# Two attention stages of a twelve-stage decoder: where TensorE sends the turned results and the turned maxima

## The chip, the cores and the metric

The program runs on one core of a Trainium2 chip. Five engines of the core are used: TensorE (matrix products, into PSUM), VectorE, ScalarE, GpSimd, and SyncE, which issues most of the DMAs. Each works through its own list of instructions in order and waits at semaphores. PSUM has eight banks of 128 x 512 words. The metric is the device time of one execution, in microseconds (us); 4994.01 is the median of three runs, from 4988.22 to 5001.19.

## The reference, cut to what matters

Twelve sub-layers follow one another, each added to x and normalized. The change touches the eighth (cross-attention to a memory, with a key mask) and the eleventh (attention over the context and x's own tokens). Both take queries from x (8 batches of 256 tokens, 128 features):

```python
def _L2_xattn_ref(memory, query, seq_mask, b):      # 8 heads of 16
    ...
    logits = jnp.einsum('bhqd,bhkd->bhqk', Q, K) + b[0]
    logits = logits + -1e+30 * (1.0 - mask)
    weights = jax.nn.softmax(logits, axis=-1)
    out = jnp.einsum('bhqk,bhkd->bhqd', weights, V)

def _L3_xattn_ref(x, context, w_qkv, w_proj, b_proj):  # 16 heads of 8
    ...
    k = jnp.concatenate([extra_k, k], axis=2)
    v = jnp.concatenate([extra_v, v], axis=2)
    attn = jnp.einsum('bhnd,bhmd->bhnm', q * scale, k).astype(jnp.float32)
    attn = jax.nn.softmax(attn, axis=-1).astype(dtype)
    out = jnp.einsum('bhnm,bhmd->bhnd', attn, v)
    return out.transpose(0, 2, 1, 3).reshape(B, N, C) @ w_proj.T + b_proj
```

The memory and the context are the same array of 1601 rows per batch. So there are 1601 keys in the first of the two and 1601 + 256 = 1857 in the second.

## The kernel before, in words

Every stage of the program ends before the next begins. Both attention stages are run by one class, `KeyMajorAttention`; below they are called memory (stage 7) and crossself (stage 10). Heads are taken in groups of four: 16 groups in memory, 32 in crossself.

A group has two parts. The first finds the largest score of each query, so that the softmax can subtract it. TensorE computes the scores with the queries on the partitions, and VectorE reduces them along the keys. That is cut into 24 *looks* per group (`pe_look`, L2315, and `dve_look`, L2462, L2465, L2469). An even look takes a slice of keys of two heads into PSUM banks 4 and 5; an odd look takes what is left of one head or of both into bank 7. After a group's 24th look VectorE splits the maxima into three parts of lower precision (`dve_split`, L2476 to L2485); TensorE *turns* them, so that they lie in rows (`pe_turn_max`, L2343, into bank 7); ScalarE copies the rows out (`act_rows`, L2425); and SyncE sends them by DMA into the stack of queries (`sp_rows`, L2289).

The second part goes over the keys in *steps* of 128: 13 steps in memory, 15 in crossself. In a step TensorE computes the scores of four heads with the keys on the partitions, the negated maxima included (`pe_scores`, L2369); ScalarE takes the exponential (L2444); TensorE multiplies with V and a column of ones (`pe_values`, L2388), summing over the steps in bank 6. After the last step ScalarE copies the sums (`act_take`, L2432), TensorE turns them back (`pe_back`, L2353, two products into bank 7), and VectorE divides and writes the result (`dve_out`, L2494 and L2495).

The looks of one group run among the steps of the group before. `looks_by(half)` says how many looks have been sent by a half step, 36 at the start, then 24 per group. In a step TensorE sends the scores of step u, some looks, the product with V of step u - 1, and some looks. In crossself a step has one or two looks (24 in 15 steps), in memory two in most.

Three things share bank 7: the odd looks, the turned maxima and the turned results. `wait_misc` (L2331) makes TensorE wait, before it writes there, until ScalarE has copied the last turned maxima and VectorE has taken the last turned result. `pe_turn_max` and `pe_back` also wait until VectorE has reduced the last odd look (`alone_done`). A look waits until VectorE has reduced the one two before it.

TensorE turns the maxima of group g at the end of the step `turn_step(g)`, and the result of group g at the end of step (g + 1) x steps + 2, each behind that step's looks. VectorE takes the turned result at the end of the same step, and ScalarE copies the turned maxima behind the exponential of step `turn_step(g)`.

Of the kernel before, what the change touches and what calls it, by code (L numbers as in the profile page):

```python
# [36 lines left out]
class Chain:  # L37


    def __init__(self, eng, sem):  # L40
        self.eng, self.sem, self.n = eng, sem, 0
# [157 lines left out]
class GroupNorm:  # L199
# [22 lines left out]
    def run_dve(self, dve, link, take):  # L222
        for g in range(4):
            if take:
                link(take(g))
            for t in range(4 * g, 4 * g + 4):
                ins = dve.bn_stats(self.stats[:, t, :], self.x[:, t, :])  # L227
            link(ins)
            for t in range(4 * g, 4 * g + 4):
                ins = dve.bn_aggr(self.moments[:, t, :], self.stats[:, t, :])  # L230
            link(ins)
            c = slice(4 * g, 4 * g + 4)
            dve.tensor_scalar(self.var[:, c], self.moments[:, c, 1], self.eps, None, ALU.add).then_inc(self.var_ready, 1)
            if g:
                self.dve_scale(dve, link, g - 1)
        self.dve_scale(dve, link, 3)
        for t in range(self.by_act, NT):
            dve.tensor_scalar(self.x[:, t, :], self.x[:, t, :], self.moments[:, t, 0:1], self.rstd[:, t:t + 1],
                              ALU.subtract, ALU.mult).then_inc(self.normed_dve, 1)
# [42 lines left out]
    def run_pe(self, pe, banks):  # L282
        if self.last:
            return
        for g in range(4):
            self.wait_normed(pe, g)
            for t in range(4 * g, 4 * g + 4):
                ins = pe.transpose(self.env.ps[:, banks[g], (t % 4) * P:(t % 4 + 1) * P], self.x[:, t, :],
                                   self.env.ident[:, :])
            ins.then_inc(self.turned, 1)  # L290
# [1891 lines left out]
class KeyMajorAttention:  # L2182


    def __init__(self, st, heads, hd, rows, lanes, tiles, nk, out_of):


        self.env, self.nc, self.ps = st.env, st.nc, st.env.ps
        self.heads, self.hd, self.rows, self.lanes, self.tiles, self.nk, self.out_of = (heads, hd, rows, lanes, tiles,
                                                                                       nk, out_of)  # L2190
        self.steps = len(tiles)
        self.per_batch = heads // 4
        self.groups = B * self.per_batch
        self.looks = 24
        self.lead = 12
        self.moves = lanes
        self.units = self.groups // lanes
        c = -(-2 * nk // 9)
        self.both = [(i * c, (i + 1) * c) for i in range(3)]
        self.alone, self.left_over = (3 * c, 4 * c), (4 * c, nk)  # L2200
        self.kst = st.sb("kst", [P, 4, 4, nk], BF16)
        self.qst = st.sb("qst", [P, 4, 4, S], BF16)
        self.v = st.sb("v", [P, 2, self.steps, D])
        self.vh = st.sb("vh", [P, 2, self.steps, heads, hd + 1])
        self.prob = st.sb("prob", [P, 3, 4 * S])
        self.oT = st.sb("oT", [P, S])
        self.part_max = st.sb("part_max", [P, 2, 8, 5])
        self.nmax = st.sb("nmax", [P, 8])
        self.left = st.sb("left", [P, 8])
        self.parts = st.sb("parts", [P, 24], BF16)  # L2210
        self.max_rows = st.sb("max_rows", [32, P], BF16)
        self.rsum = st.sb("rsum", [P, 2, 4])
        self.ones = st.sb("ones", [32, nk], BF16)
        names = ("ones_ready", "ones_loaded", "v_loaded", "v_ready", "stacks_loaded", "s_ready", "s_free", "split_ready", "turned_max",
                 "rows_ready", "max_loaded", "st_ready", "exp_done", "pv_done", "o_copied", "back_turned", "out_done",
                 "bank_clear", "dve_own")
        self.sem = {n: st.sem(n) for n in names}
        self.ident_h = st.sb("ident_h", [P, P], BF16)

    def base(self, h):  # L2220
        return 64 * (h % 2) if self.lanes == 2 else 0
# [16 lines left out]
    def turn_step(self, g):  # L2238

        return g * self.steps - self.lead * self.steps // self.looks + 2  # L2240


    def run_pool(self, pool, spans):
# [148 lines left out]

    def run_pe(self, pe):
        total = self.groups * self.steps
        turns = {self.turn_step(g): g for g in range(1, self.groups)}
        backs = {(g + 1) * self.steps + 2: g for g in range(self.groups - 1)}
        self.turned = self.backed = 0
        pe.wait_ge(self.sem["ones_loaded"], 4 * 2 * 16)
        for n in range(self.looks):
            self.pe_look(pe, n)  # L2400
        self.pe_turn_max(pe, 0)
        for n in range(self.looks, self.looks_by(0)):
            self.pe_look(pe, n)
        for u in range(total):
            self.pe_scores(pe, u)
            for n in range(self.looks_by(2 * u), self.looks_by(2 * u + 1)):
                self.pe_look(pe, n)
            if u:
                self.pe_values(pe, u - 1)
            for n in range(self.looks_by(2 * u + 1), self.looks_by(2 * u + 2)):  # L2410
                self.pe_look(pe, n)
            if u in turns:
                self.pe_turn_max(pe, turns[u])
            if u in backs:
                self.pe_back(pe, backs[u])
        self.pe_values(pe, total - 1)
        self.pe_back(pe, self.groups - 1)

# [80 lines left out]
    def run_dve(self, dve):  # L2499
        s = self.sem  # L2500
        link = Chain(dve, s["dve_own"])
        dve.tensor_copy(self.ident_h[:, :], self.env.ident[:, :])
        dve.memset(self.ps[:, 6, :], 0.0).then_inc(s["bank_clear"], 1)
        dve.wait_ge(s["bank_clear"], 1)
        total = self.groups * self.steps
        backs = {(g + 1) * self.steps + 2: g for g in range(self.groups - 1)}

        def look(n):
            self.dve_look(dve, n)
            if n % self.looks == self.looks - 1:  # L2510
                self.dve_split(dve, link, n // self.looks)
        for n in range(self.looks_by(0)):
            look(n)
        for u in range(total):
            for n in range(self.looks_by(2 * u), self.looks_by(2 * u + 2)):
                look(n)
            if u in backs:
                self.dve_out(dve, link, backs[u])
        self.dve_out(dve, link, self.groups - 1)


# [1949 lines left out]
```

## Time and profile before

| | |
|---|---|
| median of three runs | 4994.01 us |
| profiled execution | 4985.95 us |
| its span, from first to last instruction | 4984.1 us |
| mean granted clock of TensorE | 0.890 of full speed |
| TensorE busy | 4023.9 us (81%), 29194 products |
| VectorE busy | 3487.3 us (70%) |
| ScalarE busy | 2467.5 us (50%) |
| GpSimd busy | 1335.3 us (27%) |
| L2315 on TensorE, the looks | 431.3 us, 1920 products |
| L2388 on TensorE, products with V | 430.7 us, 5504 records |
| L2369 on TensorE, scores | 345.9 us, 2752 products |
| L2462 on VectorE, even looks | 564.7 us, 576 instructions |
| L2444 on ScalarE, exponentials | 703.9 us, 688 instructions |

The shares are over all twelve stages. The rows further down are cut to the two stages: memory runs from about 3380 to 3760 us after the start, crossself's attention from about 4180 to 4830. A line's time is busy time, whether it lies on the path that sets the end or not; what an engine stands for is shown in brackets behind its next instruction.

### The profile page before, as it was taken

How to read it: one execution, taken by the hardware profiler on the slowest of the kernel's cores; microseconds unless marked ns; L12 is line 12 of the kernel's file. 1: busy time of each engine (PE TensorE's matmuls, PEld its weight loads, DVE VectorE, ACT ScalarE, POOL GpSimd, SP SyncE). 2: the span in 40 equal slices, each digit the busy share in tenths (PEclk: the TensorE clock that was granted, in tenths of full speed). 3: DMA queues.
4: the chain of work that ended last, by engine and by line, in shares of the span. 5: the costliest groups of instructions: out<-in, count | busy, mean ns of one | idle time of the engine just before them, and what ended most of it. 6: DMA issues, size and time to landing. Idle time of an engine off the chain costs nothing. (4 is left out here: it accounts for less than half of the span.)

```text
span 4984.1 us, 77257 instructions
## 1 busy us (share of the span) xinstructions
PE 4023.9 (81%) x29194; PEld 2215.1 (44%) x29259; DVE 3487.3 (70%) x5453; ACT 2467.5 (50%) x3477; POOL 1335.3 (27%) x984
## 2 busy tenths in 40 slices
PE   5640787999999999999986995866996677888883
PEld 3630345666666666666653332432443342222231
DVE  6569554777777777777774445766774558888868
ACT  2120224666666666666652223543664354777772
POOL 0000001656666665666675203000000100000000
PEclk5565898999999999999997996987997688999996
DMA  0010510000000000000004106315650333323200
GB/s 19 1 53 0 105 60 27 1 14 14 1 14 1 14 1 14 1 14 1 1 1 154 37 0 152 54 15 102 86 80 4 91 59 64 56 49 56 49 2 9
DMA packets 145927, 184.01 MB, mean 37 GB/s; under 512 B 21562, under 2 KB 110156, under 8 KB 144932
## 3 DMA queue, kind: packets, MB, share of 16 engines
q1 hardware_dynamic: 137860, 162.65, 15.8%
q0 software_dynamic: 6528, 16.42, 1.4%
q8 instruction: 233, 3.82, 0.3%
q14 instruction: 122, 1.00, 0.1%
q10 hardware_dynamic: 1184, 0.12, 0.0%
HBM read 141.04 MB, written 35.08 MB: 35 GB/s over the span
## 5 line engine op out<-in xcount | busy, mean ns | idle before, releaser
L2993 POOL TENSOR_TENSOR arena<-arena 128x512 f32<-128x512 f32 (+1 forms) x768 | 1132.7, 1477 | 692.0 <-ACT arena L2949 638.7
L2444 ACT ACTIVATE arena<-ps 128x1024 f32<-128x1024 f32 (+1 forms) x688 | 703.9, 1024 | 313.1 <-PE ps L2369 302.6
L2462 DVE TENSOR_REDUCE arena<-ps 128x2 f32<-128x826 f32 (+1 forms) x576 | 564.7, 980 | 165.9 <-PE ps L2315 157.5
L3009 DVE TENSOR_TENSOR arena<-arena 128x1024 f32<-128x1024 f32 (+1 forms) x448 | 646.6, 1482 | 13.9 <-ACT arena L2976 13.9
L3031 DVE TENSOR_TENSOR arena<-ps,arena 128x512 f32<-128x512 f32 (+1 forms) x768 | 530.1, 690 | 177.3 <-ACT arena L2943 144.3
L2315 PE MATMUL ps<-arena 48*128 48x413 bf16 (+3 forms) x1920 | 431.3, 330 | 130.2 <-DVE arena L2462 65.7
L2943 ACT ACTIVATE arena<-ps 128x1024 f32<-128x1024 f32 (+1 forms) x448 | 410.5, 960 | 205.2 <-PE ps L2871 193.5
L2855 PE MATMUL ps<-arena 128*128 128x256 f32 (+1 forms) x1664 | 444.0, 392 | 20.6 <-DVE arena L3017 19.3
L2949 ACT ACTIVATE arena<-arena 128x1024 f32<-128x1024 f32 (+1 forms) x448 | 424.9, 992 | 50.8 <-DVE arena L3009 48.3
L2388 PE MATMUL ps<-arena 128*9 128x256 f32 (+2 forms) x5504 | 430.7, 384 | 11.4 <-ACT arena L2432 8.5
L2871 PE MATMUL ps<-arena 64*128 64x256 f32 (+1 forms) x3328 | 427.6, 391 | 5.6 <-ACT arena L2965 1.3
L2885 PE MATMUL ps<-arena 128*64 128x256 f32 (+1 forms) x3328 | 411.6, 388 | 7.1 <-ACT arena L2949 7.1
L2847 PE MATMUL ps<-arena 128*128 128x400 f32 (+1 forms) x1024 | 400.6, 514 | 2.9 <-ACT arena L2971 2.8
L2871 PEld LDWEIGHTS ps<-arena 64*128 64x128 f32 (+1 forms) x3328 | 301.4, 182 | 149.7 <-issue 94.8
L2855 PEld LDWEIGHTS ps<-arena 128*128 128x128 f32 (+1 forms) x1664 | 282.4, 185 | 154.5 <-issue 61.4
L2369 PE MATMUL ps<-arena 51*128 51x256 bf16 (+3 forms) x2752 | 345.9, 274 | 1.8 <-DMA arena<-arena 1.7
L2315 PEld LDWEIGHTS ps<-arena 48*128 48x128 bf16 (+1 forms) x1920 | 126.4, 95 | 453.0 <-DVE arena L2462 231.4
L2885 PEld LDWEIGHTS ps<-arena 128*64 128x64 f32 (+1 forms) x3328 | 220.4, 137 | 172.2 <-issue 85.3
L2263 POOL COPY arena<-arena 128x1536 f32<-128x1536 f32 (+2 forms) x40 | 30.1, 786 | 909.7 <-DMA arena<-arena 502.3
L2965 ACT ACTIVATE arena<-ps 128x400 f32<-128x400 f32 (+1 forms) x256 | 129.4, 506 | 257.0 <-PE ps L2847 257.0
L2847 PEld LDWEIGHTS ps<-arena 128*128 128x128 f32 x1024 | 182.6, 190 | 127.3 <-ACT arena L2971 14.2
L3041 DVE RECIPROCAL arena<-ps 128x256 f32<-128x256 f32 x64 | 112.5, 1757 | 151.8 <-PE ps L2926 151.8
(637 smaller groups left out, 5710.1 us busy)
## 6 DMA issues: line engine op xcount, KB each, us to landing
arena<-ctx_parts SPq DMA_DIRECT2D x96, 200.1 KB
arena<-ctx_parts SPq DMA_DIRECT2D x192, 100.1 KB
arena<-fs_rows SPq DMA_DIRECT2D x128, 128.0 KB, 4.1
arena<-in_ctx_feat SPq DMA_DIRECT2D x8, 1601.0 KB, 6.4
arena<-in_ctx SPq DMA_DIRECT2D x16, 768.0 KB
arena<-diff_att_stack SPq DMA_DIRECT2D x60, 192.0 KB
ctx_parts<-arena SPq DMA_DIRECT2D x24, 400.2 KB, 3.5
arena<-in_w SPq DMA_DIRECT2D x1, 6416.0 KB, 18.4
```

Of the source, the lines that this page charges most:

```text
L2315: return pe.matmul(self.ps[:, bank, c0:c0 + hi - lo], self.qst[r0:r1, ring, self.slot(g, h), q * P:(q + 1) * P], self.kst[r0:r1, ring, sel ...
L2388: ins = pe.matmul(self.ps[32 * k:32 * k + self.hd + 1, 6, 0:S], self.vh[0:rows, b % 2, t, h0 + k, :], self.prob[0:rows, u % 3, k % 2 * 2 * ...
L2444: act.activation(self.prob[0:rows, u % 3, :], self.ps[0:rows, 2 * (u % 2):2 * (u % 2) + 2, :].rearrange("p n c -> p (n c)"), ACT.Exp).then ...
L2462: ins = dve.tensor_reduce(dst[:, :, j // 2], self.ps[:, 4:6, 0:hi - lo], AX.X, ALU.max)
L2847: ins = pe.matmul(ps[:, bank, 0:hi - lo], W("wk")[:, half * INNER + u % HP * P:half * INNER + u % HP * P + P], ctxT[:, u // HP % 2, half, ...
L2855: ins = pe.matmul(ps[0:rows, bank, 0:2 * P], ctxT[:, g // 4 % 2, half, c0:c0 + rows], W("wv")[:, half * INNER + g % 4 * 2 * P:half * INNER ...
L2871: ins = pe.matmul(ps[0:rows, 2 + 2 * (s % 2) + e, t % 2 * S:(t % 2 + 1) * S], kT[e * HW:(e + 1) * HW, u % 2, c0:c0 + rows], q[e * HW:(e + ...
L2885: ins = pe.matmul(ps[e * HW:(e + 1) * HW, 6 + u % 2, 0:S], v[0:rows, u // 2 % 2, t, c0:c0 + HW], sc[0:rows, u % 2, t, e * S:(e + 1) * S], ...
L2949: act.activation(e, e, ACT.Exp).then_inc(exp_done, 1)
L2993: pool.tensor_tensor(acc[0:rows, u % 2, :], before, sc[0:rows, u % 2, t, :], ALU.add).then_inc(added, 1)
L3009: dve.tensor_tensor(e, e, mb[0:rows, u % 2, None, :].to_broadcast([rows, n, 2 * S]), ALU.subtract).then_inc(sub_done, 1)
L3031: ins = dve.tensor_tensor(most, got, most, ALU.max)
```

## The change

The places where the turns are sent are now keyed by a look, not by a step. `turn_at` and `back_at` map the number of an even look to a group, and the number is the first even one at or behind the place of the old rule. TensorE sends the turn directly behind that look, and VectorE takes the turned result directly behind its reduction of the same look. Where that look would lie beyond the last one of the stage, the old places stay (`late_turns`, `late_backs`). `run_act`, and with it the place where ScalarE copies the turned maxima, has no changed line.

```diff
+        total = self.groups * self.looks
+        pair_from = lambda n: n + n % 2
+        self.turn_at = {pair_from(self.looks_by(2 * self.turn_step(g) + 2)): g for g in range(1, self.groups)}
+        self.back_at = {pair_from(self.looks_by(2 * self.back_step(g) + 1)): g for g in range(self.groups - 1)}
+        self.late_turns = {self.turn_step(g): g for n, g in self.turn_at.items() if n >= total}
+        self.late_backs = {self.back_step(g): g for g in range(self.groups - 1)
+                           if pair_from(self.looks_by(2 * self.back_step(g) + 1)) >= total}
...
+    def back_step(self, g):
+
+        return (g + 1) * self.steps + 2
...
     def run_pe(self, pe):
         total = self.groups * self.steps
-        turns = {self.turn_step(g): g for g in range(1, self.groups)}
-        backs = {(g + 1) * self.steps + 2: g for g in range(self.groups - 1)}
...
+        def look(n):
+            self.pe_look(pe, n)
+            if n in self.turn_at:
+                self.pe_turn_max(pe, self.turn_at[n])
+            if n in self.back_at:
+                self.pe_back(pe, self.back_at[n])
...
             if u:
                 self.pe_values(pe, u - 1)
             for n in range(self.looks_by(2 * u + 1), self.looks_by(2 * u + 2)):
-                self.pe_look(pe, n)
-            if u in turns:
-                self.pe_turn_max(pe, turns[u])
-            if u in backs:
-                self.pe_back(pe, backs[u])
+                look(n)
+            if u in self.late_turns:
+                self.pe_turn_max(pe, self.late_turns[u])
+            if u in self.late_backs:
+                self.pe_back(pe, self.late_backs[u])
...
         def look(n):
             self.dve_look(dve, n)
             if n % self.looks == self.looks - 1:
                 self.dve_split(dve, link, n // self.looks)
+            if n in self.back_at:
+                self.dve_out(dve, link, self.back_at[n])
...
-            if u in backs:
-                self.dve_out(dve, link, backs[u])
+            if u in self.late_backs:
+                self.dve_out(dve, link, self.late_backs[u])
```

The new lines move the lines of these functions by 11 to 17: L2315 becomes L2326, L2343 becomes L2354, L2353 becomes L2364, L2369 becomes L2380, L2388 becomes L2399. The order of TensorE at three places, before and after, follows. In each row stand the line, the operation and the shape of what is written; 24x128 is the turn of the maxima, `x2` with 413 or 356 columns an even look.

TensorE in memory, around the turn of the maxima of the first moved group; before:

```order
L2388 MATMUL ps<-arena 17x256 x4
L2315 MATMUL ps<-arena 128x177 x2
L2343 MATMUL ps<-arena 24x128
L2369 MATMUL ps<-arena 128x256 x4
L2315 MATMUL ps<-arena 128x356 x2
```

and after:

```order
L2399 MATMUL ps<-arena 17x256 x4
L2326 MATMUL ps<-arena 128x177 x2
L2380 MATMUL ps<-arena 128x256 x4
L2326 MATMUL ps<-arena 128x356 x2
L2354 MATMUL ps<-arena 24x128
```

The turn has moved behind the next step's scores and one even look. That is so in 14 groups.

TensorE in crossself, around the turn of the maxima; before:

```order
L2388 MATMUL ps<-arena 9x256 x4
L2315 MATMUL ps<-arena 128x413 x2
L2343 MATMUL ps<-arena 24x128
L2369 MATMUL ps<-arena 128x256 x4
L2315 MATMUL ps<-arena 128x205 x2
L2388 MATMUL ps<-arena 9x256 x4
L2315 MATMUL ps<-arena 128x413 x2
```

and after:

```order
L2399 MATMUL ps<-arena 9x256 x4
L2326 MATMUL ps<-arena 128x413 x2
L2380 MATMUL ps<-arena 128x256 x4
L2326 MATMUL ps<-arena 128x205 x2
L2399 MATMUL ps<-arena 9x256 x4
L2326 MATMUL ps<-arena 128x413 x2
L2354 MATMUL ps<-arena 24x128
```

Here it stood behind an even look already, and has moved behind the next one, past the scores of a step, an odd look, a product with V and an even look. That is so in 30 groups.

TensorE in crossself, around the turned result (128x128 x2); before:

```order
L2315 MATMUL ps<-arena 128x413
L2388 MATMUL ps<-arena 9x256 x4
L2353 MATMUL ps<-ident,arena 128x128 x2
L2369 MATMUL ps<-arena 128x256 x4
L2315 MATMUL ps<-arena 128x413 x2
L2388 MATMUL ps<-arena 9x256 x4
L2315 MATMUL ps<-arena 128x205 x2
```

and after:

```order
L2326 MATMUL ps<-arena 128x413
L2399 MATMUL ps<-arena 9x256 x4
L2380 MATMUL ps<-arena 128x256 x4
L2326 MATMUL ps<-arena 128x413 x2
L2364 MATMUL ps<-ident,arena 128x128 x2
L2399 MATMUL ps<-arena 9x256 x4
L2326 MATMUL ps<-arena 128x205 x2
```

It has moved past the scores of a step and an even look, in 30 groups; on VectorE the division and the write of the result have moved behind that look's reduction. In memory the turned result stood behind an even look already, and stays there. ScalarE's, GpSimd's and SyncE's orders are the same before and after.

## Rows read from the trace of the kernel before

**Rows 1.** Busy by stretch, crossself then memory: PE, PEld, DVE, ACT, POOL; clock; DMA.

```profile
4200.00:4700.00 500.00, 439.86 (x5164) 147.63 (x5160) 445.10 (x719) 364.27 (x393) 12.32 (x18) 1.00 0.30 51
3450.00:3740.00 290.00, 266.82 (x2553) 123.97 (x2551) 226.53 (x400) 177.39 (x192) 10.23 (x12) 1.00 0.58 82
```

**Rows 2.** Who waited for whom, memory's first, then crossself's: us, times, longest.

```profile
PE ps L2343 <- DVE arena L2469: 10.0, 14, 0.7
...
PEld ps L2388 <- ACT arena L2444: 45.9, 140, 0.8
...
PE ps L2353 <- DVE arena L2465: 22.3, 30, 0.7
...
PEld ps L2369 <- DMA arena<-arena: 2.7, 4, 1.2
```

**Rows 3.** In order of time, memory: start, us, engine, [idle before <- releaser].

```profile
3552.05 0.63 PE L2388 MATMUL ps<-arena 128*17 128x256 f32 x8
...
3553.60 0.63 PE L2388 MATMUL ps<-arena 128*17 128x256 f32 x8
...
3554.53 0.53 DVE L2469 TENSOR_REDUCE arena<-ps 128x2 f32<-128x354 f32 x1
...
3555.20 0.22 PE L2343 MATMUL ps<-arena 128*24 128x128 bf16 x1 [0.71 <-DVE arena L2469]
...
3556.20 0.63 PE L2388 MATMUL ps<-arena 128*17 128x256 f32 x8
3556.30 0.90 DVE L2462 TENSOR_REDUCE arena<-ps 128x2 f32<-128x712 f32 x1 [1.25 <-PE ps L2315]
```

**Rows 4.** The same view, crossself, around the turn of the maxima.

```profile
4319.87 1.02 ACT L2444 ACTIVATE arena<-ps 128x1024 f32<-128x1024 f32 x1 [1.49 <-PE ps L2369]
4320.32 0.35 PE L2315 MATMUL ps<-arena 48*128 48x413 bf16 x2
...
4320.59 0.23 PE L2343 MATMUL ps<-arena 128*24 128x128 bf16 x1
4320.71 1.02 DVE L2462 TENSOR_REDUCE arena<-ps 128x2 f32<-128x826 f32 x1 [0.37 <-PE ps L2315]
...
4320.86 0.27 ACT L2425 ACTIVATE arena<-ps 24x128 bf16<-24x128 f32 x1
...
4322.71 0.62 PE L2388 MATMUL ps<-arena 128*9 128x256 f32 x8
...
4323.51 0.35 PE L2315 MATMUL ps<-arena 48*128 48x413 bf16 x2
...
4323.90 1.02 DVE L2462 TENSOR_REDUCE arena<-ps 128x2 f32<-128x826 f32 x1
```

**Rows 5.** The same view, around a turned result: crossself, the last row memory.

```profile
4307.34 1.02 DVE L2462 TENSOR_REDUCE arena<-ps 128x2 f32<-128x826 f32 x1
...
4308.27 0.58 DVE L2465 TENSOR_REDUCE arena<-ps 128x1 f32<-128x413 f32 x1
...
4309.00 0.41 PE L2353 MATMUL ps<-ident,arena 128*128 128x128 f32 x2 [0.74 <-DVE arena L2465]
...
4309.44 0.21 DVE L2494 RECIPROCAL arena<-ps 128x8 f32<-128x8 f32 x1 [0.59 <-PE ps L2353]
...
4310.89 0.58 DVE L2469 TENSOR_REDUCE arena<-ps 128x2 f32<-128x410 f32 x1
...
3566.59 0.53 DVE L2469 TENSOR_REDUCE arena<-ps 128x2 f32<-128x354 f32 x1 [0.50 <-PE ps L2315]
```

**Rows 6.** The same view, crossself: the maxima's DMA (SyncE's queue), a group's first scores.

```profile
4321.15 1.44 SPq L2289 DMA_DIRECT2D arena<-arena  x2
...
4325.81 0.28 PE L2369 MATMUL ps<-arena 51*128 51x256 bf16 x1
...
4344.45 1.50 SPq L2289 DMA_DIRECT2D arena<-arena  x2
...
4349.25 0.39 PE L2369 MATMUL ps<-arena 51*128 51x256 bf16 x4 [0.99 <-DMA arena<-arena]
```

More of the change, by code:

```diff
@@ L2394, in run_pe @@
         total = self.groups * self.steps
-        turns = {self.turn_step(g): g for g in range(1, self.groups)}
-        backs = {(g + 1) * self.steps + 2: g for g in range(self.groups - 1)}
         self.turned = self.backed = 0
         pe.wait_ge(self.sem["ones_loaded"], 4 * 2 * 16)
+        def look(n):
[4 more added lines that the diff above has]
+                self.pe_back(pe, self.back_at[n])
         for n in range(self.looks):
-            self.pe_look(pe, n)
+            look(n)
         self.pe_turn_max(pe, 0)
         for n in range(self.looks, self.looks_by(0)):
-            self.pe_look(pe, n)
+            look(n)
         for u in range(total):
@@ L2406, in run_pe @@
             for n in range(self.looks_by(2 * u), self.looks_by(2 * u + 1)):
-                self.pe_look(pe, n)
+                look(n)
             if u:
@@ L2410, in run_pe @@
             for n in range(self.looks_by(2 * u + 1), self.looks_by(2 * u + 2)):
-                self.pe_look(pe, n)
-            if u in turns:
-                self.pe_turn_max(pe, turns[u])
-            if u in backs:
-                self.pe_back(pe, backs[u])
+                look(n)
+            if u in self.late_turns:
+                self.pe_turn_max(pe, self.late_turns[u])
+            if u in self.late_backs:
+                self.pe_back(pe, self.late_backs[u])
         self.pe_values(pe, total - 1)
@@ L2505, in run_dve @@
         total = self.groups * self.steps
-        backs = {(g + 1) * self.steps + 2: g for g in range(self.groups - 1)}
         def look(n):
```

## The prediction

> **What bounds the kernel now.** I read the busy time by stretch first, since the share over the whole span mixes twelve stages and only two are touched. In the middle of the crossself stage VectorE is busy 445 of 500 us and TensorE 440, with the clock at its full level (1.00, that is 2.4 GHz); in the middle of the memory stage TensorE is busy 267 of 290 and VectorE 227 [rows 1]. So in crossself two engines hand work to each other with little slack on either, and in memory TensorE leads. ScalarE, 364 of 500 and 177 of 290, looks free; below it decides the result.
>
> Second, the waits, for the four hand-overs that the diff moves. Memory: TensorE stood 10.0 us in 14 places before the turn of the maxima (L2343), because the look just ahead of it was one of bank 7 and VectorE had still to reduce it [rows 2]. Crossself: TensorE stood 22.3 us in 30 places before the turn of the result (L2353) for the same reason, and the sums of the score products with V (L2388) were held by ScalarE's exponential 140 times, 45.9 us in all [rows 2]. That last row says that in crossself an exponential is often only just in time. The stand-still ahead of L2343 in crossself isn't there: it already follows a look at two heads.
>
> Third, the instructions in order of time at one place of each kind [rows 3 to 5]. In what follows S is four score products (L2369), V four products with V (L2388), a look is one L2315 step, "pair" if at two heads (banks 4 and 5), "single" if into bank 7. A number behind S, V or exp is the step of the stage, behind a look the number of the look.
>
> **The change, part by part.** 14 turns of the maxima move in memory, 30 in crossself, and 30 turned results in crossself; the turned results in memory, the first turn and the last of each kind stay where they were. No instruction is added or removed, and ScalarE's, GpSimd's and SyncE's orders are untouched. ScalarE therefore still asks for the turned maxima straight behind the exponential of the old step (step 9 of a group in memory, 10 in crossself), while TensorE now sends them a step later. That mismatch is the core of my forecast.
>
> *Memory, turn of maxima.* Now: V8 at 3553.60, look 53 (single), its reduction 3554.53 to 3555.06, turn at 3555.20 after 0.71 of standing, then S10, look 54, V9 at 3556.20; VectorE stands 1.25 us until 3556.30 [rows 3]. From V8 to V9 are 2.60 us; without a turn, V7 to V8, it is 1.55 [rows 3]. After: S10 and look 54 go ahead of the turn. Look 54 needs look 52 reduced, which it is about when VectorE begins look 53 (3554.53), so behind S10 it goes out at about 3554.76 and ends at 3555.23; the turn, 0.22 us, then finds look 53 reduced and ends at 3555.44. V9 starts at about 3555.38 instead of 3556.20: 0.82 us earlier. ScalarE copies the maxima from 3555.48 for 0.27 (duration in rows 4), then does exp 10 from 3555.80 to 3556.82; V10 wants it at V9 + 1.55 = 3556.93. It is just in time, so the exponential costs nothing here, with 0.1 us to spare. 14 x 0.82 = 11.5 us gained. Ends: 1.05 each if all of the excess goes (14.7), 0.60 if exp 10 is 0.2 late (8.4). I take 11.5.
>
> *Crossself, turn of maxima.* Now: exp 10 runs from 4319.87 to 4320.89; look 52 goes out at 4320.32, the turn at 4320.59, and ScalarE copies at 4320.86, without standing. exp 11 follows at once and V11 starts at 4322.71; look 56, queued behind it, at 4323.51, and VectorE takes that at 4323.90 [rows 4]. After: up to look 52 all is the same. Then S11, look 53 and V10, which needs exp 10, so 4321.0 to 4321.62. Look 54 needs look 52 reduced (4320.71 + 1.02 = 4321.73): 4321.80. The turn behind it needs look 53 reduced; VectorE starts that 0.93 behind look 52 (a pair's successor starts 0.93 behind it in rows 5: 4307.34, 4308.27) and takes 0.58, so it ends at 4322.22 and the turn runs from 4322.36 to 4322.59, 1.77 us later than now. ScalarE, done with exp 10 at 4320.89, stands until 4322.62, copies for 0.27, and only then does exp 11, though its scores lay ready from about 4320.95: 4322.95 to 4323.97. Behind the waiting copy every later exponential is queued, and V11 waits for the first: 4324.08 against 4322.71, 1.37 us late. S13 and look 56 stand in TensorE's queue behind V11, look 56 0.80 behind it as now, so 4324.88, and VectorE takes it at 4325.27 against 4323.90: 1.37 late as well. VectorE did look 54 without standing, and look 55 ends at about 4323.7, so it stands 1.6 us there. exp 12 follows exp 11, so V12 is late by the same. All three engines leave this place 1.37 late, and nothing behind it makes that good, since in the rest of the group they run at the pace of rows 4. 30 x 1.37 = 41 us lost. Ends: 1.00 if a stand like VectorE's 0.37 at 4320.71 [rows 4] gives its length back (30), 1.77 if the whole lateness of the turn counts (53). I take 41.
>
> *Crossself, turned result.* Now: VectorE has done look 63 (single) at 4308.85, TensorE turns the result at 4309.00, VectorE stands 0.59 for it, divides, and takes look 65 (single, two looks on) at 4310.89 [rows 5]. After: S18 and look 64 go ahead of the turn, which still runs at 4309.00; VectorE does look 64 from 4308.82 without standing, and the result from 4309.76 to 4310.23. But look 65 goes into the bank from which the result is read, so TensorE holds it until then; this order the memory stage has already, and there VectorE stands 0.50 before the single look behind the result [rows 5]. So look 65 starts at about 4310.76, 0.13 earlier than now: the 0.59 goes, 0.50 comes. 30 x 0.13 = 4 us gained. Ends: 17.7 gained if the new wait is hidden, nothing if the next pair gains nothing.
>
> *Maxima into the stack.* The copy is followed by two DMAs on SyncE's queue, and the first S of the group (S15) needs them landed. In a group that didn't wait they were issued at 4321.15 and S15 went out at 4325.81, so they landed within 4.66; in one that waited it took from 4344.45 to 4349.25, 4.80, and the first S stood 0.99 [rows 6]. The copy moves back by 1.76 and S15 by 1.37, so 0.4 of that room goes. Between 0 and 30 x 0.4 = 12 us; I take 3, since only groups near 4.7 can pay. In memory the copy stays where it is and what follows moves forward by 0.8, so the room shrinks by that: between 0 and 14 x 0.8 = 11 us. It is one DMA instead of two there, so I take nothing.
>
> *Sum:* -11.5 + 41 - 4 + 3 = 28.5 us longer. The profiled execution took 4985.95, so 5014.5 by it; it was 8 under the median of the runs shown (4994.01), and the forecast is against the median: about 5022.
>
> **The rivals.** *VectorE's gaps decide (faster).* By this, what is filled on the busiest engine is gained, and ScalarE, at 73%, absorbs its wait. Then 1.04 of the 1.25 us goes in memory (14 x 1.04 = 14.6) and 0.59 in crossself (30 x 0.59 = 17.7), the turn in crossself costs nothing, and the time is 4994 - 32 = 4962. For it: VectorE is the busiest in crossself. It decides only if ScalarE's wait is shorter than what an exponential has to spare ahead of its V, and in crossself that is nothing (45.9 us of V held by it) against 1.73 of standing. Chance 0.09. The Trainium skill, Perfetto Trace Analysis, sections "Identifying the Most-Contended Engine" and "Optimization Strategy", has this as its rule: judge VectorE and ScalarE by occupancy, and close the gaps on the most occupied. By that rule the change is a gain; the rows of this trace speak against it here, since the engine that will be late is the third busiest.
>
> *The loss is made good in part (no change).* If the pace behind the turn has 0.8 us to give (VectorE stands some 0.2 to 0.4 now and again, as at 4320.71 in rows 4), the turn costs 0.5: 15 - 15.5, so 4994. Against it: these stand-stills follow TensorE, which is late as well. Chance 0.12.
>
> *The maxima land too late (slower still).* If landing takes 5.3 us from the issue in most groups, S15, which comes 4.2 behind it, stands about 1.0 in each: 4994 + 25 + 30 = 5049. For it: the wait of 0.99. Against it: only 4 of the 30 groups stood for this DMA at all [rows 2]. Chance 0.07.
>
> **How the numbers follow.** Forecast 0.72, rivals 0.09, 0.12 and 0.07. About 0.3%, 15 us, is what a measurement of this kernel can tell from no change. The forecast's own range, with its terms not all at the same end, is 5003 to 5043 (all at their ends it would be -2 to +68 us on 4994: -14.7 + 30.0 - 17.7 + 0, and -8.4 + 53.0 + 0 + 12 + 11 with memory's DMA). The range that holds 8 in 10 leaves out the faster rival and half of the others: 4998 to 5045. Slower by over 15 us: most of the forecast (0.69), the late landing (0.07) and a little of the third, 0.79; within: 0.12; faster: 0.09.
>
> **What would show it.** In the profile after: ScalarE standing about 1.7 us ahead of the copy of the maxima (L2425 before the change) in 30 places of crossself, where it doesn't stand now [rows 4]; V in TensorE's queue held by it; a single look of VectorE behind the result standing 0.5. In memory TensorE's 0.71 ahead of the turn and most of VectorE's 1.25 behind it go. The crossself stage should be some 40 us longer and the memory stage some 11 shorter. The forecast is wrong if crossself isn't longer, above all if the exponential behind the copy starts no later than now.

## The result and the profile after

| | before | after |
|---|---|---|
| median of 4 runs each, us | 4991.11 (4983.06 to 5001.19) | 5036.32 (5029.06 to 5047.63) |
| profiled execution, us | 4985.95 | 5029.06 |
| span of its trace, us | 4984.1 | 5027.2 |
| mean granted clock of the span | 0.890 | 0.880 |

The change makes the kernel slower by 0.92%: ratio 1.0092, 95% interval 1.0064 to 1.0119. The forecast was 5022 us and its range 4998 to 5045. In what follows ratios and their intervals are of fast runs alone; one of the seven runs of e_best, 6734.61 us at a clock of 0.56, was slow and counts only in its median.

First the place of the loss. The turns of the maxima are marks that both traces have, and the first one of crossself (of its group 0) and the last one weren't moved. The same view, TensorE in order of time; of before:

```profile
4143.30 0.28 PE L2343 MATMUL ps<-arena 128*24 128x128 bf16 x1 [2.16 <-DVE arena L2485]
...
4816.92 0.22 PE L2343 MATMUL ps<-arena 128*24 128x128 bf16 x1
```

and of after:

```profile
4126.13 0.28 PE L2354 MATMUL ps<-arena 128*24 128x128 bf16 x1 [2.16 <-DVE arena L2501]
...
4860.11 0.22 PE L2354 MATMUL ps<-arena 128*24 128x128 bf16 x1
```

Up to the first turn of crossself the kernel is 17.2 us earlier than before (15.7 of it between memory's first turn and its last), and from the first turn to the last it takes 734.0 instead of 673.6 us, 60.4 more. Together that is 43.2, and the spans differ by 43.1: the whole difference lies here.

Next the stretches of [rows 1] in after, and behind them two single groups of crossself, from turn to turn (columns: PE, PEld, DVE, ACT, POOL; clock; DMA):

```profile
3450.00:3740.00 290.00, 277.97 (x2694) 130.94 (x2691) 234.80 (x419) 185.33 (x203) 10.22 (x12) 1.00 0.57 82
4200.00:4700.00 500.00, 433.91 (x4759) 142.44 (x4757) 412.97 (x665) 332.99 (x364) 10.23 (x15) 0.93 0.27 45
4306.65:4328.92 22.27, 19.03 (x224) 6.44 (x224) 19.24 (x32) 15.55 (x17) 0.00 (x0) 1.00 0.01 2
4228.50:4257.40 28.90, 27.52 (x224) 7.97 (x224) 19.75 (x32) 15.74 (x17) 0.00 (x0) 0.65 0.57 90
```

In memory TensorE's busy time rises from 267 to 278 of 290 us: about half of its standing has gone. In crossself VectorE falls from 445 to 413 of 500, and the granted clock falls from 1.00 to 0.93. The last two rows show what the 0.93 is made of: the same 224 matmuls take 22.27 us from turn to turn in one group, at a clock of 1.00, and 28.90 in another, at 0.65. So two things have to be told apart in crossself: what a group takes at the full clock, and how many groups don't have it. From turn to turn a group takes, at the full clock (the value that most of the groups show):

| us per group | before | after | difference | groups | product |
|---|---|---|---|---|---|
| memory | 22.40 | 21.46 | -0.94 | 14 | -13.2 |
| crossself | 21.46 | 22.27 | +0.81 | 30 | +24.3 |

The memory row is a little less than the 15.7 us of the marks: in before two more groups took 23.70, in after none does. Of the 60.4 us that crossself takes longer, 24.3 are this pace. The other 36.1 are a net sum of groups that are longer than the pace. In after those are the intervals at a low clock: of the 30 between the first moved turn and the last turn 12 have a mean clock under 1.00 (0.65 to 0.94), and together they are 41 us longer than 12 groups of 22.27. In before one is at 0.93, and all that exceeds the pace in these intervals comes to some 5 us.

Then the waits of crossself in after, to be read against [rows 2] (the view begins behind the first moved turn):

```profile
PEld ps L2399 <- ACT arena L2460: 74.9, 208, 0.8
...
ACT arena L2441 <- PE ps L2354: 50.7, 29, 2.4
...
PE ps L2399 <- ACT arena L2460: 17.0, 38, 0.5
...
PE ps L2354 <- DVE arena L2485: 6.5, 28, 0.2
...
PE ps L2364 <- DVE arena L2481: 5.5, 25, 0.2
```

TensorE's 22.3 us ahead of the turned result have become 5.5, as the change would have it. In their place ScalarE stands 50.7 us in 29 places ahead of its copy of the maxima (L2441), where it stood once, for 0.6, and the products with V are held by its exponential: the loading of their weights (PEld) for 74.9 us instead of 45.9, and the products themselves (PE) for 17.0 in 38 places, where before has 1.9 in 9 (the row below). TensorE also has a new wait of 0.23 ahead of the moved turn, 6.5 us in all, for VectorE. The view has no row in which the scores (L2380) wait for the maxima's DMA, which [rows 2] had four times.

```profile
PE ps L2388 <- ACT arena L2444: 1.9, 9, 0.3
```

Now one place of each kind in order of time. Crossself around the turn of the maxima, in after (start, us, engine):

```profile
4326.32 0.62 PE L2399 MATMUL ps<-arena 128*9 128x256 f32 x8
...
4328.92 0.22 PE L2354 MATMUL ps<-arena 128*24 128x128 bf16 x1 [0.23 <-DVE arena L2485]
...
4329.17 0.27 ACT L2441 ACTIVATE arena<-ps 24x128 bf16<-24x128 f32 x1 [1.72 <-PE ps L2354]
4329.35 3.06 ACT L2460 ACTIVATE arena<-ps 128x1024 f32<-128x1024 f32 x3
...
4329.54 0.33 PE L2326 MATMUL ps<-arena 48*128 48x413 bf16 x1
...
4330.40 0.62 PE L2399 MATMUL ps<-arena 128*9 128x256 f32 x8 [0.53 <-ACT arena L2460]
...
4331.56 1.02 DVE L2478 TENSOR_REDUCE arena<-ps 128x2 f32<-128x826 f32 x1 [1.06 <-PE ps L2326]
```

The first row is V9, the last product ahead of the moved turn but one. ScalarE's copy starts 1.72 late, the exponentials queue behind it (three of them run on end, since their scores lay ready), V11 stands 0.53 for the first, and VectorE 1.06 for the look queued behind V11.

Memory around the turn, in after, to be read against [rows 3]:

```profile
3547.58 0.63 PE L2399 MATMUL ps<-arena 128*17 128x256 f32 x8
...
3549.18 0.22 PE L2354 MATMUL ps<-arena 128*24 128x128 bf16 x1
...
3549.19 0.64 PE L2399 MATMUL ps<-arena 128*17 128x256 f32 x8
3549.24 0.90 DVE L2478 TENSOR_REDUCE arena<-ps 128x2 f32<-128x712 f32 x1 [0.21 <-PE ps L2326]
3549.43 0.27 ACT L2441 ACTIVATE arena<-ps 24x128 bf16<-24x128 f32 x1 [1.03 <-PE ps L2354]
...
3550.85 0.63 PE L2399 MATMUL ps<-arena 128*17 128x256 f32 x8
```

TensorE doesn't stand ahead of the turn, VectorE stands 0.21 instead of 1.25, and from V8 to V9 are 1.61 us where 2.60 stood, and 1.66 to the next.

Crossself around a turned result, in after, to be read against [rows 5]:

```profile
4315.13 0.58 DVE L2481 TENSOR_REDUCE arena<-ps 128x1 f32<-128x413 f32 x1
...
4315.66 1.02 DVE L2478 TENSOR_REDUCE arena<-ps 128x2 f32<-128x826 f32 x1
...
4315.85 0.41 PE L2364 MATMUL ps<-ident,arena 128*128 128x128 f32 x2 [0.23 <-DVE arena L2481]
...
4316.60 0.20 DVE L2510 RECIPROCAL arena<-ps 128x8 f32<-128x8 f32 x1
...
4317.58 0.59 DVE L2485 TENSOR_REDUCE arena<-ps 128x2 f32<-128x410 f32 x1 [0.52 <-PE ps L2326]
```

VectorE goes from one look to the next and into the division without standing; the single look behind it stands 0.52.

Last, what happens ahead of a fall of the clock. TensorE in after, in the group of 28.90 us above:

```profile
4228.50 0.22 PE L2354 MATMUL ps<-arena 128*24 128x128 bf16 x1 [0.23 <-DVE arena L2485]
...
4229.97 0.62 PE L2399 MATMUL ps<-arena 128*9 128x256 f32 x8 [0.53 <-ACT arena L2460]
...
4231.03 1.04 PE L2399 MATMUL ps<-arena 65*9 65x256 f32 x8
...
4233.23 1.04 PE L2399 MATMUL ps<-arena 128*9 128x256 f32 x8
```

Behind the 0.53 us in which V is held, the next V takes 1.04 instead of 0.62: from there the engine runs at 1.2 GHz (from 4231.5 to 4250 the granted clock reads 0.50). Ten of the 12 intervals lose their clock like this: it falls 1.6 to 2.8 us behind the turn, and V is held from 0.95 to 1.48 behind it, and it stays at 0.50 for 6.8 to 20.5 us. The other two share one fall, at the end of a group, behind a look for which TensorE stood 1.35; before has a fall at the same place, and it is shorter (3.4 us instead of 13.7).

### The profile page after: what moved, and what is told of

The parts are those of the page before. It is cut to its first block and busy times, and to the rows that moved or that the text cites. A ratio compares the mean times of both kernels' runs of the same rounds, so it can differ in the third digit from the quotient of the medians.

```text
span 5027.2 us, 77322 instructions
## 1 busy us (share of the span) xinstructions
PE 4078.9 (81%) x29259; PEld 2225.5 (44%) x29259; DVE 3488.4 (69%) x5453; ACT 2459.9 (49%) x3477; POOL 1333.8 (27%) x984
## 3 DMA queue, kind: packets, MB, share of 16 engines
q1 hardware_dynamic: 137860, 162.65, 15.7%
## 5 line engine op out<-in xcount | busy, mean ns | idle before, releaser
L2326 PE MATMUL ps<-arena 48*128 48x413 bf16 (+3 forms) x1920 | 450.3, 342 | 141.2 <-DVE arena L2478 67.7
L2399 PE MATMUL ps<-arena 128*9 128x256 f32 (+2 forms) x5504 | 453.3, 403 | 24.0 <-ACT arena L2460 17.9
L2872 PE MATMUL ps<-arena 128*128 128x256 f32 (+1 forms) x1664 | 444.0, 392 | 20.5 <-DVE arena L3034 19.2
L2966 ACT ACTIVATE arena<-arena 128x1024 f32<-128x1024 f32 (+1 forms) x448 | 425.0, 992 | 50.7 <-DVE arena L3026 48.2
L2380 PE MATMUL ps<-arena 51*128 51x256 bf16 (+3 forms) x2752 | 362.0, 285 | 0.0
L2326 PEld LDWEIGHTS ps<-arena 48*128 48x128 bf16 (+1 forms) x1920 | 135.5, 97 | 477.0 <-DVE arena L2478 240.3
L2380 PEld LDWEIGHTS ps<-arena 51*128 51x128 bf16 (+3 forms) x2752 | 174.5, 100 | 108.9 <-issue 63.0
```

Source lines behind the costliest of these rows:

```text
L2326: return pe.matmul(self.ps[:, bank, c0:c0 + hi - lo], self.qst[r0:r1, ring, self.slot(g, h), q * P:(q + 1) * P], self.kst[r0:r1, ring, sel ...
L2380: ins = pe.matmul(self.ps[0:rows, 2 * (u % 2) + k % 2, k // 2 * S:(k // 2 + 1) * S], self.kst[r0:r1, ring, self.slot(g, k), c:c + rows], s ...
L2399: ins = pe.matmul(self.ps[32 * k:32 * k + self.hd + 1, 6, 0:S], self.vh[0:rows, b % 2, t, h0 + k, :], self.prob[0:rows, u % 3, k % 2 * 2 * ...
L2872: ins = pe.matmul(ps[0:rows, bank, 0:2 * P], ctxT[:, g // 4 % 2, half, c0:c0 + rows], W("wv")[:, half * INNER + g % 4 * 2 * P:half * INNER ...
```

## The experiments

The theory: the crossself turn of the maxima alone costs, because ScalarE's order wasn't changed with it, and the falls of the clock come from the standing that this brings into TensorE. The rivals: the loss comes from the turned result or from late maxima, and the falls have a cause of their own. Each ratio is to runs of the kernel before on the same chip, with its 95% interval. The first three kernels do one part of the change each; in all of them a part is undone by a line behind the tables of moved steps (`lanes` is 1 in memory, 2 in crossself).

**e_mem: only memory's turn is moved.**

```diff
+        if lanes == 2:
+            self.turn_at, self.late_turns = {}, {self.turn_step(g): g for g in range(1, self.groups)}
+        if lanes == 2:
+            self.back_at, self.late_backs = {}, {self.back_step(g): g for g in range(self.groups - 1)}
```

Expected:

> The kernel before with one part of the change: only memory's 14 turns of the maxima move. Wait theory: memory's groups go from 22.40 to 21.46 us as in the trace after, so about 13 us faster than before (4978 on 4991), crossself unchanged at 21.46 per group with the clock at 1.00. Rival, all of the loss lies in the memory stage's later effects on the loads: no gain, or slower.

Measured: 4981.08 against 5002.96 us, ratio 0.9958 (0.9945 to 0.9971): 14 to 28 us faster. A group of memory takes 21.46, one of crossself 21.46 as before. The memory part is a gain, and no smaller than its -13.2. In two groups of crossself the clock falls here too (0.81 and 0.86 on average); TensorE stood there 2.7 and 1.7 us for the maxima's DMA.

**e_back: only crossself's turned results are moved.**

```diff
+        if lanes == 1:
+            self.turn_at, self.late_turns = {}, {self.turn_step(g): g for g in range(1, self.groups)}
+        if lanes == 2:
+            self.turn_at, self.late_turns = {}, {self.turn_step(g): g for g in range(1, self.groups)}
```

Expected:

> The kernel before with only crossself's 30 turned results moved. Theory that ScalarE's copy costs the time: this part is harmless, 0.1 to 0.3 us per group gained, 4 to 9 us in all (4982 to 4987), clock 1.00 in crossself. Rival, the result's wait that now stands ahead of the single look costs the time: 0.5 us per group and more, 15 us or more slower (5006 and up).

Measured: 4997.87 against 5002.96, ratio 0.9993 (0.9983 to 1.0002). Two consecutive turns, in order of time:

```profile
4278.67 0.23 PE L2358 MATMUL ps<-arena 128*24 128x128 bf16 x1
...
4299.84 0.23 PE L2358 MATMUL ps<-arena 128*24 128x128 bf16 x1
```

That is 21.17 us, 0.29 less than before, or 9 us in 30 groups; the timing alone can't tell it from nothing, the pace in the trace can. The turned result doesn't cost.

**e_turn: only crossself's turn of the maxima is moved.**

```diff
+        if lanes == 1:
+            self.turn_at, self.late_turns = {}, {self.turn_step(g): g for g in range(1, self.groups)}
+        if lanes == 2:
+            self.back_at, self.late_backs = {}, {self.back_step(g): g for g in range(self.groups - 1)}
```

Expected:

> The kernel before with only crossself's 30 turns of the maxima moved. Theory that ScalarE's copy costs the time: V behind it 1.1 us late in 30 groups, 34 us slower, and if the clock falls come with that standing, some 30 more: 5050 to 5060, clock well under 1.00 in crossself. Rival, the copy's wait alone and the clock falls belong to something else: 34 us slower, 5025, clock 1.00 in crossself. Rival, the result's turn is the cause: within 10 us of 4991.

Measured: 5060.22 against 5002.96, ratio 1.0123 (1.0107 to 1.0139): 53 to 70 us slower. That is more than the whole change (1.0092), though the intervals overlap. Two turns in order of time:

```profile
4295.67 0.22 PE L2358 MATMUL ps<-arena 128*24 128x128 bf16 x1 [0.23 <-DVE arena L2489]
...
4318.24 0.22 PE L2358 MATMUL ps<-arena 128*24 128x128 bf16 x1 [0.23 <-DVE arena L2489]
```

A group at the full clock takes 22.57, that is +1.11, or 33 us in 30 groups. With the turned result's -0.29 this gives +0.82, and after has +0.81: the two add up. What is over the 33 us goes with the clock, 0.94 from 4200 to 4750 us where before has 1.00: 11 of the 30 intervals are under 1.00, and nine of them lose their clock 1.7 to 2.3 us behind the turn. The interval behind the second row shows that this doesn't need the loads of keys that run in the 28.90 us group above (DMA 0.57); here the DMA share is 0.01 and the clock 0.86:

```profile
4318.24:4343.39 25.15, 22.03 (x223) 6.96 (x224) 19.53 (x32) 15.74 (x17) 0.00 (x0) 0.86 0.01 2
```

**e_act: the change, with ScalarE's copy of the maxima moved back by one step as well**, so that the exponential of the next step goes ahead of it.

```diff
-        turns = {self.turn_step(g): g for g in range(1, self.groups)}
+        late = 1 if self.lanes == 2 else 0
+        turns = {self.turn_step(g) + (late if self.turn_step(g) not in self.late_turns else 0): g
+                 for g in range(1, self.groups)}
```

Expected:

> The changed kernel with ScalarE's copy of the maxima behind the exponential of the next step in crossself (step 11 of a group instead of 10), so that it isn't asked for a step before TensorE sends it. Theory that the early copy costs the time: ScalarE's 1.72 us of standing in 30 groups go, the clock stays at 1.00 in crossself, and the time is 4991 - 13 - 4 to 9, about 4970. Rival, the later turn itself costs it (a later landing of the maxima, the single look held by the copy): still 20 us or more over 4991.

Measured: 5004.7 against 5002.96, ratio 1.0007 (0.9996 to 1.0018). Against the change (1.0092, 1.0064 to 1.0119) that gives back about 0.85%, and the intervals don't meet: ScalarE's order is a cause, and the larger one by the paces below. But of the two forecasts, 20 us faster than before and 20 slower, neither came true; the gain of memory isn't left over, so it isn't the only cause. Two rows of the waits of crossself, and a place in order of time:

```profile
ACT arena L2441 <- PE ps L2354: 19.4, 29, 0.7
...
PE ps L2380 <- DMA arena<-arena: 13.6, 9, 3.6
```

```profile
4317.09 0.35 PE L2326 MATMUL ps<-arena 48*128 48x413 bf16 x2 [0.18 <-DVE arena L2480]
...
4317.67 0.22 PE L2354 MATMUL ps<-arena 128*24 128x128 bf16 x1 [0.23 <-DVE arena L2487]
4317.82 0.41 PE L2380 MATMUL ps<-arena 51*65 51x256 bf16 x4
...
4317.93 0.27 ACT L2441 ACTIVATE arena<-ps 24x128 bf16<-24x128 f32 x1 [0.67 <-PE ps L2354]
...
4318.29 0.33 PE L2326 MATMUL ps<-arena 48*128 48x413 bf16 x1
4318.55 0.62 PE L2399 MATMUL ps<-arena 128*9 128x256 f32 x8
```

ScalarE stands 0.67 instead of 1.72, and V11 isn't held by an exponential any more. A group takes 21.68 at the full clock: of the turn's 1.11 (22.57 less 21.46), 0.59 were ScalarE's order (22.27 less 21.68), and 0.51 stay (21.68 less 21.17). For these the rows show three candidates, all waits that come with the turn's new place. TensorE stands 0.18 for VectorE ahead of the even look and 0.23 for VectorE ahead of the turn; before has neither. And the single look ahead of V11 starts 0.47 behind the scores (4317.82 to 4318.29), where before has 0.22 (4322.22 to 4322.44): it goes into bank 7, where the turned maxima lie until the copy ends at 4318.20, and V11 is queued behind it. No kernel took one of these waits away by itself, so how the 0.51 divides among them isn't shown.

The rival of late maxima, which the change itself doesn't show, shows here: 9 groups stand for the maxima's DMA, up to 3.60 us. (TensorE stands for it now and then in other kernels too: four groups in before, two in e_mem, five in e_back; each number is of one trace.) And all six intervals of e_act with a mean clock under 1.00 hold one of these waits: without V held there, the clock doesn't fall at the turn. These groups are most of what e_act is still behind: from the first turn to the last crossself takes 33 us longer than in before (706.65 instead of 673.62), and the pace is only 6.6 of it (30 x 0.22).

**e_fill: the change, with TensorE kept at work where V is held.** In 30 groups of crossself the four score products two steps behind the turn's step are sent twice, the second time behind the single look. The second time they write the same numbers to the same place.

```diff
+            twice = self.lanes == 2 and u - 2 in filled
-            self.pe_scores(pe, u)
+            self.pe_scores(pe, u, not twice)
             for n in range(self.looks_by(2 * u), self.looks_by(2 * u + 1)):
                 look(n)
+            if twice:
+                self.pe_scores(pe, u)
```

Here `filled` holds the steps of the moved turns, and the new argument of `pe_scores` says whether the scores are reported to ScalarE.

Expected:

> The changed kernel, with the four score products of step 12 of each of 30 groups in crossself sent twice, the second time behind the single look, where TensorE stands 0.53 us for ScalarE (same result). Theory that TensorE's standing there brings its clock down: the stretches at the lower level get fewer though no wait is shorter, and the time falls by 10 to 35 us against the changed kernel. Rival, the falls of the clock have another cause: 0 to 10 us slower than the changed kernel, group of 22.27 us or a little more, as many stretches at the lower level.

Measured: 5004.49 against 4995.69, ratio 1.0011 (1.0000 to 1.0022). A stretch of crossself, and a place in order of time:

```profile
4200.00:4750.00 550.00, 472.68 (x5540) 161.78 (x5536) 470.35 (x760) 378.88 (x414) 12.30 (x18) 1.00 0.30 49
```

```profile
4299.75 0.27 ACT L2446 ACTIVATE arena<-ps 24x128 bf16<-24x128 f32 x1 [1.72 <-PE ps L2354]
...
4300.12 0.55 PE L2380 MATMUL ps<-arena 51*65 51x256 bf16 x4
...
4300.97 0.62 PE L2400 MATMUL ps<-arena 128*9 128x256 f32 x8 [0.31 <-ACT arena L2465]
```

ScalarE stands 1.72 as in the change, and a group takes the same 22.27. What differs is that TensorE stands 0.31 ahead of V instead of 0.53, and that the clock over the stretch is 1.00 and not 0.93: three intervals between turns have less than 1.00, not 12, and none of the three loses its clock behind V (one does right behind a wait of 1.20 for the maxima's DMA, and two share the fall at the end of a group that before has too). More work, sent for nothing, makes the kernel 0.8% faster (1.0011 against 1.0092, about 40 us; the intervals don't meet), a little more than the 10 to 35 us expected. By the two traces it is 29 us from crossself's first turn to its last (705.22 instead of 733.98). So the falls of the clock behind V cost some 30 to 40 us, and they come from what TensorE does, or doesn't, at this place.

**e_fill0: the kernel before, with the same products sent twice.**

```diff
-            self.pe_scores(pe, u)
+            twice = self.lanes == 2 and u - 2 in filled
+            self.pe_scores(pe, u, not twice)
```

Expected:

> The kernel before with the same 30 x 4 score products sent twice at the same place, where TensorE doesn't stand: the price of the filling alone. Both theories: 0.25 to 0.4 us in each of 30 groups, 8 to 12 us slower than before, clock 1.00 in crossself.

Measured: 5002.83 against 4995.69, ratio 1.0009 (0.9993 to 1.0026); 21.66 a group, +0.20, under the 0.25 to 0.4 expected. Where nothing stands the filling costs a little, so what it gives in e_fill isn't a gain that every order of the work would have had.

**e_gap: the kernel before, with the exponential behind the turn made late by itself.** Behind ScalarE's copy of the maxima it does five more small copies that nobody reads; no instruction is moved.

```diff
         act.activation(self.max_rows[0:24, :], self.ps[0:24, 7, 0:P], ACT.Copy).then_inc(s["rows_ready"], 1)
+        if self.lanes == 2 and 0 < g < self.groups - 1:
+            for k in range(5):
+                act.activation(self.idle_rows[0:24, k, :], self.ones[0:24, 0:P], ACT.Copy)
```

Expected:

> The kernel before, all of TensorE's and VectorE's order untouched, with five small copies (24x128) on ScalarE behind the copy of the maxima in 30 groups of crossself, so that the next exponential starts about 1 us later (these copies' result isn't used). Theory that a TensorE held by a late exponential loses twice, by standing and by the clock: V about 0.6 us late in 30 groups, 18 us, and stretches at the lower clock on top, 30 us or more slower in all. Rival, the falls of the clock belong to the later turn and its loads: about 18 us slower with the clock at 1.00.

Measured: 5006.04 against 4995.69, ratio 1.0014 (1.0001 to 1.0028). In order of time:

```profile
4310.70 1.09 ACT L2429 ACTIVATE arena<-arena 24x128 bf16<-24x128 bf16 x5
4311.69 3.06 ACT L2448 ACTIVATE arena<-ps 128x1024 f32<-128x1024 f32 x3
...
4312.74 0.62 PE L2389 MATMUL ps<-arena 128*9 128x256 f32 x8 [0.29 <-ACT arena L2448]
```

V is held for 0.29, half of the 0.6 expected, a group takes 21.81 (+0.35, or 10 us in 30 groups), and the clock is 1.00 in every group of crossself behind the first moved turn. A late exponential by itself costs about its hold; this smaller standing didn't bring the clock down. That the falls follow from any lateness of ScalarE is thereby out; a hold of 0.53 without the moved turn wasn't tried.

**e_best: memory's turn and crossself's turned results are moved, crossself's turn of the maxima is left where it was.**

```diff
+        if lanes == 2:
+            self.turn_at, self.late_turns = {}, {self.turn_step(g): g for g in range(1, self.groups)}
```

Expected:

> The kernel before with memory's 14 turns of the maxima and crossself's 30 turned results moved, and crossself's turn of the maxima left where it was. If the parts add: 0.9958 x 0.9993, about 0.995 of before, 24 us faster. Rival, the two parts don't add since the stages differ in when loads arrive: no better than memory's part alone (0.9958).

Measured: 4977.25 against 4995.69, ratio 0.9955 (0.9938 to 0.9973): 13 to 31 us faster than before, and it beats both kernels. Its groups take 21.46 in memory and 21.16 in crossself. Whether it beats e_mem (0.9958) can't be told by the intervals.

## Why the prediction came out near, and which step failed

The direction and the mechanism were right; the sum wasn't. Its terms gave +28.5, and the two traces differ by 43: crossself is 60 us longer, where I had some 40, and what lies ahead of it 17 shorter, where I had 11.

- *Crossself, turn of the maxima, +41 forecast: mis-sized.* The lateness of the turn was right: it runs 2.60 behind V9 (4328.92 less 4326.32), that is the forecast 1.77 more than the 0.83 of before, and ScalarE stands 1.72 against 1.73. The step that failed is "only then does exp 11": I put the exponential 0.33 behind the copy's start and V 1.13 behind the exponential's. Measured are 0.18 (4329.17 to 4329.35) and 1.05 (4329.35 to 4330.40). The 0.33 is the distance of before (the copy at 4320.86 [rows 4], the exponential at 4321.19), and there it wasn't the copy that held the exponential but its own scores, as more rows of before, in order of time, show (the first is V9):

```profile
4319.76 0.62 PE L2388 MATMUL ps<-arena 128*9 128x256 f32 x8
...
4320.75 0.39 PE L2369 MATMUL ps<-arena 51*128 51x256 bf16 x4
...
4321.19 1.02 ACT L2444 ACTIVATE arena<-ps 128x1024 f32<-128x1024 f32 x1
```

  The scores end at 4321.14, the copy at 4321.13. Which of the two counted, after shows: where the scores lie ready, the exponential starts while the copy is still running. The two differences make 0.23 of the 0.24 by which 1.37 was too long: from V9 to V11 are 4.08 us (4326.32 to 4330.40), where before has 2.95 (4319.76 to 4322.71), 1.13 more, and e_turn's groups have +1.11. 30 x 1.11 = 33.
- *A second cause in the same term was not seen.* I put the whole lateness on ScalarE's order. e_act shows that this is 0.59 of it, and 0.51 stay when the copy is moved too, with TensorE's new waits for VectorE (0.18 and 0.23) and for bank 7 in the rows. VectorE's standing ahead of look 56, 1.6 by my working, is 1.06: the hold was shorter, and the reduction of the single look ahead of it ended some 0.24 later than I had it.
- *Crossself, turned result, -4 forecast: the right kind, too small.* The 0.59 ahead of the division went and 0.52 ahead of the single look came, 0.50 being forecast. But from the single look ahead of the turn to the one behind the result are 2.45 instead of 2.62, 0.17 less and not 0.13, and over a group e_back has -0.29. The remaining 0.12 I haven't followed to a row. 30 x 0.29 = 9.
- *Memory, -11.5 forecast: right, a little too small.* V9 starts 0.01 behind the turn's start, and not some 0.15 as I had it; V8 to V9 are 1.61 and not 1.78, which gives 0.17 more. The next product came 0.11 later than the pace of 1.55, where I counted on none. That makes 0.88; the group shows -0.94: -13.2. The remaining 0.06 I haven't followed to a row.
- *Maxima into the stack, +3 forecast: nothing in this trace.* No group of after stood for this DMA. That isn't a rule: TensorE stood for it in four places of e_fill, where the copy has the same place (up to 1.20), and in nine of e_act, where it is later.
- *The clock, not in the sum at all.* The prediction reads [rows 1], "with the clock at its full level", and carries it over to the changed kernel as a given. This is the largest error: 36.1 us by the traces, some 30 to 40 by e_fill. The new standing on TensorE cost more than its own length here.

By the measured paces alone the change would cost 24.3 - 13.2 = 11 us, where I had 28.5. That the time fell into the range is in part luck, two errors of opposite sign: the terms of pace were put too high by 17, and the clock was left out.

Of the rivals, "VectorE's gaps decide" fell with e_turn (slower, though VectorE's wait for the turned result isn't touched there) and with the 1.06 that VectorE itself stands behind V11. The rule that I weighed with it is the Trainium skill's, in Perfetto Trace Analysis, section "Optimization Strategy": find the gaps on the engine that is to be made faster, and what they wait for. The runs agree in small: e_back, which closes such a gap of VectorE, the most occupied engine, gains 0.29 a group. The loss lay elsewhere, in the wait of the third busiest engine and in the clock. "The loss is made good in part" is true of the pace (+0.81 and not +1.24), though not by the slack that it named. "The maxima land too late" has the nearest time (5049) and the wrong cause.

What stays open: why 10 of 30 groups lose the clock behind V and the others, with the same rows around the turn, don't. The length of a standing alone doesn't decide it: before has 0.74 ahead of the turned result in each of 30 groups ([rows 5]) at a clock of 1.00. Open is also whether e_act with the filling, which wasn't tried, would be faster than before.

## What to carry to other kernels

When an instruction that another engine waits for is sent later, look at what is queued behind the waiting instruction on that engine, and move the wait with it; an engine at 73%, as ScalarE here, can set the pace if its next result is needed at once. Then ask whether the waits that come in are on TensorE: a group that stood 0.53 us where it hadn't stood before lost up to 6.6 us more to the clock. Read a pace from the groups that most often recur and list the others beside the granted clock, since an average over the stage mixes the two costs. And where one line of a change serves two stages, try it in each by itself: here the same move gained 0.94 us a group in one and lost 1.11 in the other.

## What the runs showed of the hardware

I hadn't expected TensorE's clock to fall in a stage in which the engine is busy 19.03 of 22.27 us a group. In after it fell to 1.2 GHz in 10 of 30 groups, behind a hold of V of about half a microsecond, and stayed there for 6.8 to 20.5 us; in e_act it fell only in groups that stood 1.15 us or more for the maxima's DMA; in e_gap, with 0.29 of standing, in none behind the first moved turn. Standing of 0.74 at another place of the group, in before, didn't bring it down. Sending four products twice for nothing left no fall behind V and was worth about 0.8% of the whole kernel.
